# A decoder layer with a bit-plane FFN: ScalarE's decoder blends placed ahead of its waits for TensorE, and half a decoder tile moved to the multiply stage

## The reference

```python
x = x + attn(layernorm(x))            # 32 heads, 4-bit weights: (qw - 8) * scale
x = x + xattn(layernorm(x), ctx_1024) # rat_read, attention, rat_write, then a gated multiply, rat_write
x = x + ffn(layernorm(x))             # weights decoded from bit planes
# inside xattn, second half:
mlp_in = rat_read(hidden, ...)                  # g_in, u_in
mlp_out = silu(g_in @ W0.T) * (u_in @ W1.T)     # (2, 512, 1024)
hidden = rat_write(hidden, mlp_out, ...)
# ffn: code = 4 bits from 4 planes; w[o, i] = lut4[o, code[o, i]]; y = x @ w.T + bias
```

## Time and profile before

| | us |
|---|---|
| median of 3 runs | 1802.63 |
| the profiled execution's own time | 1792.48 |
| its span | 1790.7 |
| `write_read`, from 1412 to | 1598 |
| steps 4 to 15 of the multiply, from 1544 to | 1598 |
| second write up to the first FFN product | 1598 to 1668 |
| FFN products | 1668 to 1790 |

### The profile page before, as it was taken

The page is one execution under the profiler, slowest core; times in us unless marked ns, Lnnn a source line. Parts: engine busy times, 40 slices in busy tenths (PEclk is TensorE's granted clock), DMA queues, the critical chain, the costliest instruction groups (busy, mean ns, idle before and its releaser), DMA issues. The chain is left out here.

```text
span 1790.7 us, 21054 instructions
## 1 busy us (share of the span) xinstructions
PE 1586.8 (89%) x6880; PEld 1046.3 (58%) x6880; DVE 1356.7 (76%) x2078; ACT 914.7 (51%) x1686; POOL 578.1 (32%) x463
## 2 busy tenths in 40 slices
PE   4899999999999999999999988767899767888999
PEld 3466666666666666666666655465455446445444
DVE  7688788788788788788788867586578578678881
ACT  3345455455455455455554453233458776567630
POOL 2246346446446446446446444210110100000000
PEclk9999999999999999999999999979889855898999
DMA  5001101101102102101101000050634200000121
GB/s 183 24 25 59 36 25 59 36 24 59 36 24 59 36 24 59 36 25 59 36 24 48 24 25 23 18 190 37 129 74 69 91 1 1 1 36 1 47 77 41
DMA packets 30963, 84.20 MB, mean 47 GB/s; under 512 B 6006, under 2 KB 7304, under 8 KB 30600
## 3 DMA queue, kind: packets, MB, share of 16 engines
q1 hardware_dynamic: 30856, 82.87, 15.8%
HBM read 70.27 MB, written 12.58 MB: 46 GB/s over the span
## 5 line engine op out<-in xcount | busy, mean ns | idle before, releaser
L518 DVE SCALAR_TENSOR_TENSOR acc<-pj,sc_o,acc 128x1024 f32<-128x1024 f32 x232 | 293.8, 1278 | 89.4 <-PE pj L649 86.1
L628 POOL TENSOR_TENSOR prob<-prob,inv_total 128x512 f32<-128x512 f32 (+3 forms) x256 | 189.6, 745 | 385.4 <-DVE inv_total L560 385.4
L518 DVE SCALAR_TENSOR_TENSOR q_acc<-pj,sc_q,q_acc 128x1024 f32<-128x1024 f32 x224 | 286.2, 1278 | 34.5 <-PE pj L649 29.3
L649 PE MATMUL pj<-ctx_hi,w_o 128*128 128x512 f32 x528 | 237.1, 449 | 25.5 <-ACT spare L407 12.3
L649 PE MATMUL pj<-zT_hi,w_q 128*128 128x512 f32 x512 | 225.6, 441 | 4.0 <-PEq L81 3.1
L649 PE MATMUL pj<-ctx_lo,w_o 128*128 128x512 f32 x528 | 207.9, 394 | 0.0
L461 ACT ACTIVATE prob<-ps,low_max 128x512 f32<-128x512 f32 (+3 forms) x256 | 134.1, 526 | 144.4 <-DVE low_max L553 144.3
L649 PE MATMUL pj<-zT_lo,w_q 128*128 128x512 f32 x512 | 204.5, 399 | 0.0
L703 PE MATMUL ps<-kT,qT 128*128 128x512 f32 (+3 forms) x512 | 185.7, 445 | 10.5 <-ACT prob L461 10.5
L727 PE MATMUL pv<-probT,v 128*128 128x512 f32 (+3 forms) x512 | 169.5, 433 | 0.0
L649 PEld LDWEIGHTS pj<-ctx_hi,w_o 128*128 128x128 f32 x528 | 99.1, 188 | 110.5 <-DVE acc L518 43.0
(11 more groups left out here) (338 smaller groups left out, 3141.0 us busy)
## 6 DMA issues: line engine op xcount, KB each, us to landing
raw_o<-in_w_o SPq DMA_DIRECT2D x33, 512.0 KB, 3.6
raw_q<-in_w_q SPq DMA_DIRECT2D x32, 512.0 KB, 3.6
x_ring<-qk_kept SPq DMA_DIRECT2D x64, 128.0 KB, 5.1
ln_x<-in_x SPq DMA_DIRECT2D x8, 512.0 KB, 6.9
raw_kv<-in_w_k SPq DMA_DIRECT2D x8, 512.0 KB, 3.6
raw_kv<-in_w_v SPq DMA_DIRECT2D x8, 512.0 KB, 4.6
x<-in_x SPq DMA_DIRECT2D x8, 512.0 KB, 6.6
x_kept<-x SPq DMA_DIRECT2D x8, 512.0 KB, 2.9
```

The source lines that it names most:

```text
L518: dve.scalar_tensor_tensor(out=dst, in0=pj[slot][:], scalar=scale, in1=dst, op0=ALU.mult, op1=ALU.add).then_inc(evac_v, 1)
L628: pool.tensor_tensor(prob[:, k % PROBS, 0:w], prob[:, k % PROBS, 0:w], inv_total[:, n:n + 1].to_broadcast([P, w]), ALU.mult).then_inc(norm ...
L649: ins = pe.matmul(pj[slot][:, b * S:(b + 1) * S], lhs, part[:, b * S:(b + 1) * S], start=n == 0, stop=n == 1)
```

## The change

Three tables of numbers and two loops are changed. `Q_MLP` goes from 28 to 24, so half 6 (the first half of tile 3, 4 quarters) is decoded in the multiply stage and no longer in the first write. `W1_QUARTERS` spreads the 8 quarters that stay there over the first four row tiles and leaves none for the last four. Tile 3 is turned ahead of step 10 instead of step 9. In the multiply stage and in the second write ScalarE's blends of a step stand in front of its copies and of `gated`.

```diff
-Q_W1, Q_MLP, Q_W2, Q_END = 16, 28, 48, 64
+Q_W1, Q_MLP, Q_W2, Q_END = 16, 24, 48, 64
-W1_QUARTERS = ((0, 2, 4, 5, 6, 7, 8, 8), (8, 10, 11, 12, 12, 12, 12, 12))
+W1_QUARTERS = ((0, 2, 3, 4, 5, 6, 7, 8), (8, 8, 8, 8, 8, 8, 8, 8))
-MLP_TURNS = {9: 3, 14: 4}
+MLP_TURNS = {10: 3, 14: 4}
             for n in range(MLP_IN_READ, len(STEPS)):
+                for q in range(mlp_quarter(n), mlp_quarter(n + 1)):
+                    deq.blend(act, q)
                 if n in MLP_TURNS:
                     deq.copy(act, MLP_TURNS[n], p_w, fT)
                 gated(n)
-                for q in range(mlp_quarter(n), mlp_quarter(n + 1)):
-                    deq.blend(act, q)
...
             for i in range(half + 3):
+                for q in range(w2_quarter(i), w2_quarter(i + 1)):
+                    deq.blend(act, q)
                 if 1 <= i <= half:
                     wr.copy_od(act, i - 1)
...
                 if i - 1 in W2_TURNS[0]:
                     half_tile(W2_TURNS[0][i - 1])
-                for q in range(w2_quarter(i), w2_quarter(i + 1)):
-                    deq.blend(act, q)
```

## The result

The changed kernel takes 1820.46 us, the median of 4 runs (1819.6 to 1827.6), against 1799.99 for the kernel before (4 runs, 1797.2 to 1807.58). The ratio is 1.0127 (95% interval 1.0102 to 1.0152), which on 1799.99 is 22.9 us more (18.4 to 27.4). The prediction had +23.7 on the median of the runs then shown, 1826, with a range of 1811 to 1836. The profiled execution took 1819.60 us, 27.1 more than that of before.

The account below looks back on a forecast made before the run. VectorE's row of products and merges was taken to bound the multiply stage, TensorE the FFN products. Multiply stage +27.0, first write -2.8 and second write -0.5 gave +23.7 us on 1802.63, so 1826 us, range 1811 to 1836.

Parts of the forecast that it names:

- The cycle: Multiply stage from step 6: VectorE and ScalarE wait on each other; two steps take 12.0 us instead of 9.03.
- Rival A: Multiply stage: VectorE stays dense, the Silu is never late; -2 to +2 us, 1801 to 1805; chance 0.05.
- Rival B: Both writes' early starts win and the moved half fills VectorE's waits; 10.8 us less, 1792; chance 0.03.
- Rival C: Multiply stage: TensorE idles 2.6 us a step and its clock drops, steps of 6.9 us; 1841; chance 0.07.
- Its size: Multiply-stage product intervals: 6.04 us from an even product (begins a half), 5.96 from an odd one (ends it).
- The turns: Steps 10 and 14: ScalarE's two copies and a TensorE step before the Silu add 6.30 and 4.64, 10.9 us together.
- The moved half: Multiply stage: the moved half's own merges make up 7.8 of the 27.0 us added.
- The first write: ScalarE's copy for row tile 5, and so VectorE's first update, comes 2.8 us earlier; bounds 0 and 5.6.
- The second write: copy_low of row tile 3, which TensorE's fifth row tile awaits, comes 0.5 us earlier; bounds 0 and 5.2.
- The level: Whole kernel: +23.7 us on the shown runs' median of 1802.63, predicted as 1826 us.
- Rival D: Multiply stage: handing over costs less, VectorE stands 1.5 us a pair; +16 us, 1818; chance 0.09.

Follow-up runs that it names:

- experiment 5: Changed kernel with only the tile turns spread over two steps each, blends still ahead of the Silu: 1811.74 us, ratio 1.0072 to the kernel before.
- experiment 6: Changed kernel (Q_MLP = 24, second write's new order) with Silu ahead of the blends again and turns spread over two steps: 1795.32 us, ratio 0.9987.
- experiment 4: Kernel before (Q_MLP = 28, Silu first) with the second write's new order and turns spread over two steps: 1792.87 us, ratio 0.9971.
- experiment 2: Kernel before (Q_MLP = 28) with only the order changed in steps 4 to 15, blends ahead of the Silu: 1812.78 us, ratio 1.0087.
- experiment 7: Kernel before with turns spread, second write's new order, blends ahead of the Silu and VectorE's merges ahead of its product: 1788.07 us, ratio 0.9941.
- experiment 1: Changed kernel with the Silu ahead of the blends again in steps 4 to 15: 1808.26 us, ratio 1.0058 to the kernel before.
- experiment 8: Changed kernel with, from step 5 on, one quarter's blends ahead of the Silu and one behind it: 1808.75 us, ratio 1.0054.
- experiment 3: Changed kernel with VectorE's merges of a step ahead of its product, ScalarE's order kept: 1803.25 us, ratio 1.0032 to the kernel before.

## Why the prediction was right

**The cycle.** The step of the prediction on which everything rests, merge, blends, Silu, product, merge, is what the timelines show, at the merges named. Three runs cut it at different places (order undone, VectorE swapped, the late blends behind the Silu), and the interval goes to 4.5 us in all three. Rivals A and B are out with the result, C with the intervals of 5.9.

**Its size.** Predicted 6.04 from an even and 5.96 from an odd product; measured 5.90 to 5.91 and 5.84 to 5.91 where no turn lies. The waits fit as well: about 25 us over the stage were forecast and 25.6 in ten waits measured, and no merge waits for a blend. What I mis-sized is the step from the last blend to the Silu. From rows 4 I read that a Silu begins only when the blend ahead of it has ended, 0.82 us after its start. At that place it had waited for TensorE, whose step 11 ended at 1575.25:

```profile
1571.65 3.60 PE L2025 MATMUL w1py<-inT,mlp_w 128*128 128x512 f32 x8
```

In the changed kernel the Silu starts 0.71 us after the last blend's start (1556.00 behind a blend begun at 1555.29) and takes 0.57. The ten intervals less the turns come to 58.8 us where 60.0 stand in the sum.

**The turns.** Predicted 10.9 for both; measured 12.04 - 5.86 and 12.57 - 5.86, 12.9 together, and 12.9 again as what experiment 5 takes away. I had taken one turn at the price with a slow clock and one at full clock. After standing 12 us TensorE is slow at both: 4.62 and 5.13 us for the eight matmuls that take 3.60. The two errors go against each other, -1.2 in the cycle and +2.0 in the turns (and -0.1 behind product 15), so that the stage came to 78.7 against 78.0 is in part luck.

**TensorE's clock.** Rival C supposed that TensorE would idle 2.6 us in each step. It did not. With three PSUM buffers it did steps 10 to 13 in a row from 1581.08 on, at full clock from 1585.6 to 1596 (1.00), and its idle time lies in blocks at the turns, 3.36 and 11.88 us at the first, 0.96 and 12.25 at the second. The mean granted clock from 1544 to 1626 us is 0.80 against 0.96 before, but on the path it costs only what the two steps behind the turns take above 3.60 us, 2.6 in all, and some 0.5 in the transposes ahead of each (1.11 and 1.12 against 0.66). What a rhythm of short idle times would do to the clock, no run here shows.

**The moved half.** The 7.8 us of merges that I worked out are the 7.8 between experiments 6 and 4.

**The first write.** 2.8 predicted, 2.62 at the first update and 2.94 at product 4. Of the profiles in which the second row tile ran at full clock, the other two with 12 quarters (experiments 2 and 7) have 42.20 and 42.34 us up to the update, and the other three with 8 (1, 6 and 8) 39.54 to 39.80, so the term is real. But it is made up otherwise than I argued. The softplus and the copy behind it in the changed kernel:

```profile
1440.79 1.22 ACT L1665 ACTIVATE w1e<-w1e 128x1216 f32<-128x1216 f32 x1
1441.91 0.36 ACT L1626 ACTIVATE w1sT<-w1py 128x256 f32<-128x256 f32 x1
```

The copy comes 25.84 us after the write's start, against 27.87 before: 2.0 us earlier and not 2.8. I had put the new places of the first half's blends at nothing, but the last two of them now stand between the copies ahead of the softplus, and it begins 0.8 us later (24.72 against 23.93). The other 0.6 came from TensorE's row tile 6, before and changed:

```profile
1445.18 2.12 PE L1606 MATMUL w1ph<-odT,w1sT 128*128 128x376 f32 x4
```

```profile
1446.43 1.52 PE L1606 MATMUL w1ph<-odT,w1sT 128*128 128x376 f32 x4
```

Its granted clock was 0.66 before and 0.96 now; TensorE had stood 4.57 us ahead of row tile 5 before and stood 2.68 now. I had not forecast that, so the agreement to 0.2 us is luck.

**The second write.** 0.5 predicted. The difference of the whole rest, 0.80, would not show it: over the ten profiles this rest runs from 190.6 to 192.7 us with no relation to the order. From the start of TensorE's fourth row tile to copy_low of row tile 3 it is clean. Of the changed kernel:

```profile
1647.20 1.22 PE L1606 MATMUL w2po<-odT,acc 128*128 128x376 f32 x3
```

```profile
1658.30 0.25 ACT L1639 ACTIVATE w2dlT<-w2pl 8x128 f32<-8x128 f32 x1
```

That is 11.10 us. TensorE's same row tile before:

```profile
1619.52 5.32 PE L1606 MATMUL w2po<-odT,acc 128*128 128x376 f32 x16
```

With the copy at 1631.15 it was 11.63 us. Of the first four experiments, the three with the new order have 11.09 to 11.10 us, and the one with the old order (2) has 11.65. The term is 0.5 us at this place; that it reaches the end of the kernel is not shown.

**The level.** +23.7 against 23.8 in the changed blocks; the 0.7 us more in the stage and the 0.8 less in the whole rest cancel there, so the last tenth means nothing. The time is 1820.46, not 1826: the kernel before came to 1799.99 over four runs, where I stood on 1802.63, and the measured +20.5 between medians is inside the interval of 18.4 to 27.4. Rival D (+16) lies outside it, and its pair of steps of 10.5 us is not what the timeline shows (11.8).

## What to carry to other kernels

Before moving work ahead of a wait, write down what each moved instruction itself waits for. If that is made by the engine that waits for the queue behind it, the two engines wait for each other in every step from then on, and idle time on both in the busy shares is no cover for it. What counts is how late the merge comes for which the instructions ahead of the hand-over wait, and not their number alone (experiment 8); and the cycle can be opened at either engine. A hand-over in two halves through one buffer was cheaper here laid on two steps than ahead of one: 5.9 us in the kernel before, 12.9 in the changed one.

## What the runs showed of the hardware that I had not expected

- Back to back on ScalarE, a Silu starts 0.71 us after the start of a 128x512 blend that itself takes 0.80. A start right at a predecessor's end can be another wait that ended at the same time.
- TensorE's clock differs between executions of the same instructions: the first write's second row tile took 1.43 us before and in the changed kernel (granted clock 1.00), but 2.71 in experiments 3, 4 and 5 (0.50). The update comes 43.05 and 42.76 us after the write's start in experiments 3 and 5, against 39.71 in the changed kernel with the same first write, and 44.40 in experiment 4, against 42.33 before. That is as much as the first write's whole gain, so single profiles decide a term of this size only by an interval between two rows near it.
- Idle time ahead of matmuls does not by its length alone decide the clock behind it: in the kernel before TensorE stood 2.14 us between the halves of both turns, and the eight matmuls behind took 4.84 us at the first and 3.60 at the second.
